# First attention of a vision tower: slot 0's exponential sums in halves, the last maxima behind them, and the value-weight scalings dealt out anew

## The reference, cut to what matters

```
q = einsum('bsc,oc->bso', x, Wq)      # 8 heads, 64 features each
k = einsum('bsc,oc->bos', x, Wk);  v = einsum('bsc,oc->bos', x, Wv)   # shared by the heads
scores = einsum('bhsd,bdt->bhst', q, k) / sqrt(8)
attn = softmax(scores, axis=-1)
ctx = einsum('bhst,btd->bhsd', attn, v)
out = einsum('bcp,oc->bop', ctx.transpose(0,2,1,3).reshape(b, H*KD, s), Wo)
```

## Time and profile before

| | |
|---|---|
| median of 3 runs | 71.36 us (71.33 to 71.44) |
| the profiled execution's own time | 71.47 us |
| its span, first to last instruction | 69.6 us |
| busy: TensorE / VectorE / ScalarE / GpSimd | 60.6 / 41.7 / 29.7 / 13.5 us |
| granted TensorE clock | 1.00 |
| scores of slot 0 to the end of `out0(3)` | 18.26 to 28.34 us |

### The profile page before, as it was taken

How to read it: one execution, slowest core, us unless ns; L and a number is a source line. 1 busy time by engine, 2 the same in 40 slices (tenths; PEclk the granted TensorE clock), 3 DMA queues, 4 the chain that set the end, 5 groups by cost and what they waited for, 6 DMA issues and landing times.

```text
span 69.6 us, 1990 instructions
## 1 busy us (share of the span) xinstructions
PE 60.6 (87%) x830; PEld 39.6 (57%) x839; DVE 41.7 (60%) x111; ACT 29.7 (43%) x69; POOL 13.5 (19%) x32
## 2 busy tenths in 40 slices
PE   3995896999999999999989995959999969989940
PEld 1330462787698578564448565548794318654910
DVE  2491039975699995535962546999563025756830
ACT  0240012431748852177764425259604283953030
POOL 6800039200000892058304000000000004000000
PEclk9999999999999999999999999999999999999999
DMA  0799999950000000000000000000000000000003
GB/s 0 182 381 370 392 225 243 235 175 0 0 9 0 0 0 9 0 0 5 0 0 0 0 9 5 0 9 0 0 9 0 0 0 0 0 0 0 0 0 75
DMA packets 2390, 4.07 MB, mean 58 GB/s; under 512 B 780, under 2 KB 1230, under 8 KB 2382
## 3 DMA queue, kind: packets, MB, share of 16 engines
q1 hardware_dynamic: 1568, 3.49, 17.4%
q10 hardware_dynamic: 781, 0.46, 2.2%
q0 software_dynamic: 32, 0.00, 0.0%
HBM read 3.82 MB, written 0.13 MB: 57 GB/s over the span
## 4 chain that ended last, share of the span: by engine, by line
PE 61%; DVE 12%; DMA 9%; ACT 7%; POOL 3%; issue 3%; DVEq 0%; ACTq 0%; POOLq 0%
DMA Xt<-in_x_dram 9%; PE psum L717 8%; PE psum L711 6%; DVE top L533 4%; ACT ge L457 3%; POOL WoS L300 3%; PE psum L727 3%; PE psum L928 3%; PE psum L974 3%; PE psum L819 3%; PE psum L770 3%; PE psum L1066 2%; PE psum L746 2%; DVE E L632 2%; DVE top L630 2%
## 5 line engine op out<-in xcount | busy, mean ns | idle before, releaser
L717 PE MATMUL psum<-warm 128*128 128x512 bf16 x44 | 14.5, 441 | 1.7 <-DVE warm L479 1.2
L717 PEld LDWEIGHTS psum<-warm 128*128 128x128 bf16 x53 | 5.2, 109 | 6.8 <-issue 3.6
L300 POOL TENSOR_TENSOR WoS<-pack_attn,top 128x256 f32<-128x256 f32 x5 | 3.1, 647 | 10.1 <-DVE top L540 10.1
L492 DVE TENSOR_TENSOR onehot<-idb,iota 128x2048 bf16<-128x2048 bf16 x4 | 4.8, 1241 | 0.0
L335 POOL TENSOR_TENSOR resT<-hT,xC 128x256 f32<-128x256 f32 x1 | 0.7, 724 | 20.0 <-DVE xC L661 20.0
L428 ACT ACTIVATE E<-E 128x512 f32<-128x512 f32 x4 | 2.5, 631 | 3.1 <-DVE E L632 3.1
L727 PE MATMUL psum<-Xt,pack_wp 128*64 128x256 f32 x16 | 2.2, 390 | 1.1 <-DMA Xt<-in_x_dram 1.1
L457 ACT ACTIVATE ge<-psum,pack_moe 128x512 f32<-128x512 f32 x4 | 2.5, 687 | 1.2 <-PE psum L1026 1.2
L711 PE MATMUL psum<-pack_ident,E 128*128 128x128 f32 x16 | 2.5, 276 | 0.7 <-DVE E L632 0.7
L630 DVE TENSOR_REDUCE top<-psum 128x8 f32<-128x512 f32 x4 | 2.7, 683 | 0.4 <-PE psum L943 0.4
L498 DVE TENSOR_TENSOR centre<-pack_ident,mean 128x128 f32<-128x128 f32 x1 | 0.3, 293 | 4.4 <-DMA pack_ident<-in_ident_dram 4.4
(11 more groups left out here) (206 smaller groups left out, 134.6 us busy)
## 6 DMA issues: line engine op xcount, KB each, us to landing
Xt<-in_x_dram SPq DMA_DIRECT2D x1, 1024.0 KB, 6.4
Xt<-in_x_dram SPq DMA_DIRECT2D x1, 512.0 KB, 7.4
pack_both<-in_both_dram SPq DMA_DIRECT2D x2, 240.2 KB, 8.8
pack_moe<-in_moe_dram SPq DMA_DIRECT2D x1, 450.0 KB, 9.8
pack_mid<-in_mid_dram SPq DMA_DIRECT2D x1, 327.5 KB, 9.7
pack_attn<-in_attn_dram SPq DMA_DIRECT2D x1, 288.0 KB, 8.0
pack_expert<-in_expert_dram SPq DMA_DIRECT2D x2, 130.0 KB, 9.4
pack_wp<-in_wp_dram ACTq DMA_DIRECT2D x1, 192.0 KB, 5.8
```

The source lines that it names most:

```text
L300: gp.tensor_tensor(WoS[:, s, 4 * u:4 * u + 4, :].rearrange("p (b n) d -> p b n d", b=2), bc(WoT[:, 2 * u:2 * u + 2, :], 1, 2), bc(top0[:, ...
L492: ve.tensor_tensor(onehot[:, 16 * k:16 * k + 16, :], bc(idb[:, k, :], 1, 16), iota16[:, :, :], ALU.is_equal).then_inc(s_hot, 1)
L717: mm(B[bank][:, :], lhsT=warm[:, 0:P], rhs=warm[:, :], start=True, stop=True)
```

## The change

Slot 0's eight exponentials signal after four and after eight. VectorE sums slot 0 in two halves of four heads, each with its own reciprocal, between the maxima of slot 2 and those of slot 3. So `softmax0_max(3)` stands behind both half sums. On TensorE `scores0(3)` moves behind `shift0(1)`. GpSimd scales slot 0's halves each after its own reciprocal, then both halves of slot 1, then slot 2 (first) and slot 3 (second). ScalarE scales slot 2 (second) rather than slot 1 (second), and does so after copying out slot 0's mix rather than before. VectorE keeps slot 3 (first) alone. Two of the three `keep_clock` products ahead of mix 0 go. The semaphore counts follow.

```diff
             def scaled_Wo(s, u, ready):
 
                 pool.wait_ge(s_rinv, ready)
...
-            scaled_Wo(0)
-            scaled_Wo(1)
-            scaled_Wo(2)
-            scaled_Wo(3)
+            scaled_Wo(0, 0, 1)
+            scaled_Wo(0, 1, 2)
+            scaled_Wo(1, 0, 3)
+            scaled_Wo(1, 1, 3)
+            scaled_Wo(2, 0, 4)
+            scaled_Wo(3, 1, 5)
...
-            for i in range(HEADS):
-                ins = sc.activation(E0[:, 0, i, :], B[i // 4][:, i % 4 * TOK:(i % 4 + 1) * TOK], ACT.Exp,
-                                    bias=shift[:, i:i + 1], scale=SC0)
-            ins.then_inc(s_exp0, 1)
+            for u in range(2):
+                for i in range(4 * u, 4 * u + 4):
+                    ins = sc.activation(E0[:, 0, i, :], B[i // 4][:, i % 4 * TOK:(i % 4 + 1) * TOK], ACT.Exp,
+                                        bias=shift[:, i:i + 1], scale=SC0)
+                ins.then_inc(s_exp0h, 1)
...
-            act.wait_ge(s_rinv, 2)
+            mixed(0)
+            act.wait_ge(s_rinv, 4)
             for i in range(4, HEADS):
-                ins = sc.activation(WoS[:, 1, i, :], WoT[:, 2 + i % 2, :], ACT.Copy, scale=top0[:, 2, 1, i:i + 1])
+                ins = sc.activation(WoS[:, 2, i, :], WoT[:, 2 + i % 2, :], ACT.Copy, scale=top0[:, 2, 2, i:i + 1])
             ins.then_inc(s_wosa, 1)
-            mixed(0)
...
             softmax0_max(2)
+            for u in range(2):
+                dve.wait_ge(s_exp0h, u + 1)
+                softmax0_sum(0, slice(4 * u, 4 * u + 4), u + 1)
             softmax0_max(3)
-            softmax0_sum(0)
             for s in range(1, SLOTS):
-                softmax0_sum(s)
-            for s, u in ((2, 1), (3, 0)):
-                dve.wait_ge(s_rinv, s + 1)
+                dve.wait_ge(s_exp0, s)
+                softmax0_sum(s, slice(0, HEADS), s + 2)
+            for s, u in ((3, 0),):
+                dve.wait_ge(s_rinv, 5)
...
             def mix0(s):
 
                 c, j = s // 2, s % 2
-                pe.wait_ge(s_exp0, s + 1)
-                pe.wait_ge(s_wos, s + 2)
-                if s == 1:
+                pe.wait_ge(s_wos, (2, 4, 5, 6)[s])
+                if s == 2:
                     pe.wait_ge(s_wosa, 1)
-                elif s >= 2:
-                    pe.wait_ge(s_wosd, s - 1)
+                elif s == 3:
+                    pe.wait_ge(s_wosd, 1)
...
             scores0(2)
+            shift0(1)
             scores0(3)
-            shift0(1)
             shift0(2)
             shift0(3)
+            pe.wait_ge(s_exp0h, 2)
+            keep_clock(0, 1)
+            mix0(0)
             pe.wait_ge(s_exp0, 1)
-            keep_clock(0, 3)
-            mix0(0)
-            pe.wait_ge(s_exp0, 2)
             keep_clock(2, 1)
             mix0(1)
             out0(0)
```

More of the change, by code:

```diff
@@ L210, in vit_tower @@
                                                sem("v0_ready"))
-        s_sc0, s_mx0, s_sub0, s_exp0 = sem("scores0_ps"), sem("max0_done"), sem("shifted0_ps"), sem("exp0_done")
+        s_sc0, s_mx0, s_sub0, s_exp0h, s_exp0 = (sem("scores0_ps"), sem("max0_done"), sem("shifted0_ps"), sem("exp0_half_done"),
+                                                  sem("exp0_done"))
         s_shift, s_wosa, s_gbar = sem("shift_ready"), sem("wos1_ready_act"), sem("gate_bar_ready")
@@ L294, in _, with scaled_Wo @@
                 pool.wait_ge(const_l1, 5 + u)
[L296 to L303, removed]
-            scaled_Wo(0)
-            scaled_Wo(1)
-            scaled_Wo(2)
-            scaled_Wo(3)
+            def scaled_Wo(s, u, ready):
+                pool.wait_ge(s_rinv, ready)
+                gp.tensor_tensor(WoS[:, s, 4 * u:4 * u + 4, :].rearrange("p (b n) d -> p b n d", b=2),
+                                 bc(WoT[:, 2 * u:2 * u + 2, :], 1, 2),
+                                 bc(top0[:, 2, s, 4 * u:4 * u + 4].rearrange("p (b n) -> p b n", b=2), 3, D),
+                                 ALU.mult).then_inc(s_wos, 1)
+            scaled_Wo(0, 0, 1)
[4 more added lines that the diff above has]
+            scaled_Wo(3, 1, 5)
             pool.wait_ge(in_expert, 32)
@@ L534, in softmax0_max, with softmax0_sum @@
                                  negate=True).then_inc(s_mx0, 1)
[L536 to L540, removed]
+            def softmax0_sum(s, heads, done):
+                ve.tensor_reduce(top0[:, 1, s, heads], E0[:, s, heads, :], X, ALU.add).then_inc(s_sum0, 1)
+                dve.wait_ge(s_sum0, done)
+                ve.reciprocal(top0[:, 2, s, heads], top0[:, 1, s, heads]).then_inc(s_rinv, 1)
             softmax0_max(0)
@@ L827, in out0 @@
                 pe.wait_ge(s_v0_ev, 1)
-                pe.wait_ge(s_exp0, 3)
+                pe.wait_ge(s_exp0, 2)
                 for b in range(2):
```

## The result

| | before | after |
|---|---|---|
| median | 71.40 us (71.33 to 71.47) | 72.14 us (71.96 to 72.28) |
| ratio after to before | | 1.0085 (1.0051 to 1.0119) |
| median and ratio, both kernels run again on another chip | 71.61 us | 72.03 us: 1.0064 (1.0041 to 1.0087) |
| span of the profiled execution | 69.6 us | 70.5 us |
| first product on image data | 7.26 | 7.64 |

What follows compares the result with a forecast made beforehand. Gapless TensorE work from mix 2 to the residual addition was taken to bound the kernel; mix 2, waiting for ScalarE's scalings, starts 0.33 late: 71.36 + 0.33 = 71.69, said as 71.7 us, range 71.25 to 71.95.

Steps and rivals of the forecast that it cites:

- Everything outside the stretch: Before the first maxima and from the residual addition on: nothing changes; the loss is simply added to a median of 71.36.
- The stretch: First attention, first maxima to residual addition: the addition moves from 28.46 to 28.79, 0.33 us later.
- the cost of coming back from scores 3 to shift 2: TensorE, return from 64x64 tiles to the full array: 0.10 for the mode change, then shift 2 takes 0.87.
- leaving out both drains: TensorE's two tile-mode changes around scores 3: without them the final sum would be about 0.1 smaller.
- Maxima 3 behind the half sums: VectorE: half sums of 0.42 each let maxima 3 start at 22.39; scores 3 allow the same time, taken as 22.40.
- GpSimd's head start isn't used: Before mix 0: GpSimd starts 0.97 us earlier, but TensorE arrives at 24.36 against 24.23 before.
- ScalarE ends the wait of mix 2: Mix 2: ScalarE's four scalings, behind its copy of mix 0, end at 26.31; mix 2 starts at 26.46, 0.33 late.
- At mix 1: GpSimd's two scalings of slot 1 end at 25.22; mix 1 starts at 25.37, while TensorE alone would allow 25.28.
- Rival (A): TensorE and VectorE: mode changes cost nothing and half sums don't hold the maxima; no slower, 71.43 us; chance 0.20.
- (B): Mix 1: GpSimd's two scalings of slot 1 decide at 0.78 each; mix 2 0.49 late, 71.85 us; chance 0.12.
- (C): Mix 0 and 1 use GpSimd's early start; mix 0 at 24.07, 0.16 earlier, 71.2 us; chance 0.13.
- (D): TensorE's clock drops to 1.2 GHz; the 4 us from mix 0 to out 3 take up to twice as long; chance 0.03.

Runs made afterwards that it cites:

- a_scores_first: Changed kernel with TensorE's order put back, scores 3 ahead of shift 1: ratio 1.0029 to the kernel before, first maxima to residual addition 9.63 us against 9.78.

## Why the prediction was right or wrong

The way was right, slower, and so was the chain of waits that led there. The time of 72.14 lies above the range, which ended at 71.95, and 0.45 above the forecast of 71.69. Two steps of the sum failed: the first makes up most of the error in the time, the second is the error in the stretch itself.

- *Everything outside the stretch*: the sum put it at nothing and set the loss on top of 71.36, the median of three runs within 0.11 us, with a measurement said to be good to 0.2%. The runs showed that this level isn't so steady. 27 runs of the same kernel on another chip lay between 71.36 and 72.23, with a median of 71.61, so 71.36 was at their lower end. The changed kernel had 72.03 there, again above the range. The difference between the two kernels in that comparison, 0.46, would have given 71.82. In the profiled executions of the first comparison, 0.38 of the 0.9 us are the image data landing later; for the other runs there is no profile, so what moved the medians stays open. This part is about 0.3 of the 0.45.
- *The stretch*: forecast +0.33, measured +0.43 twice. The step that failed is the cost of coming back from scores 3 to shift 2. The change of mode itself was 0.09 in (22.10 is 0.31 behind the last full product's 21.79) and close to the forecast out. But the first product after it holds the array for longer, as its 0.48 against 0.38 shows: shift 2 took 0.98 until shift 3's first product (22.72 to 23.70), not 0.87. The sum had 0.97 for shift 1, whose first product shows the same 0.48 in the earlier trace rows, and 0.87 for shift 2, though after the change it too is the first of its mode. That missing 0.1, with 0.04 of smaller differences, runs on: exponential 2 at 23.51 by the clock of before (forecast 23.37), mix 0 at 24.51 (24.36), mix 2 at 26.55 (26.46), the addition at 28.89 (28.79). ScalarE's copy followed mix 0 after 0.73, not 0.78, so 0.05 of the error was made up by luck. The Trainium skill's page "TensorEngine Tiling (Array Packing)", section Key Properties, says that a change of mode drains TensorE; the trace agrees, and here the drain with its slower first product was about 0.2 us per way back. The prediction's "about 0.1" for leaving out both drains doesn't follow from its own rows: without them shift 3 would have waited for maxima 3 until about 23.12 instead of 23.18, so its sum would have been 0.06 smaller.
- *Maxima 3 behind the half sums*: right, and scores 3 held them as well, as the forecast had it, in the end 0.1 longer. Half sums took 0.41 and 0.42 (0.42 forecast). The Trainium skill's page "VectorE: DVE Perf Modes", section on the TRN2 errata, gave an estimate of 0.33 by its row for an SBUF source, which the same section says comes out too low; the measured value agrees with that.
- *GpSimd's head start isn't used*: right, 1.0 us early, and 1.4 us of waiting for TensorE.
- *ScalarE ends the wait of mix 2*: right. The row says so, and taking two heads away gave back 0.23. What TensorE itself would have allowed was forecast at 0.21 earlier (26.25 against 26.46). At mix 1, where GpSimd was to come last by 0.09, TensorE's own list and GpSimd's scaling ended together: mix 1 stands 0.32 behind its `keep_clock` product, as mix 0 does with 0.31.
- *Rival (A)* fell with the mode changes of 0.09 and the half sums of 0.41, *(B)* because GpSimd's scalings of slot 1 ran at 0.57 and 0.61 each, *(C)* because TensorE reached mix 0 later than before, at 24.51 and not at 24.07, so that GpSimd's early scalings lay waiting, *(D)* because the stretch kept the full clock.

## What to carry to other kernels

A step that frees one engine early is worth nothing if the consumer's own list reaches the result later than before: read the list of the consumer first, then the time of the producer. Moving work ahead on an engine that feeds a chain (here half sums ahead of the last maxima) costs the whole chain behind it; the same half sums one place later were one of three parts of a version that gained 0.42 there. Which part gave how much wasn't measured. A forecast of an absolute time also needs the spread of the level that it starts from: about 0.3 of the 0.45 us of error came from there. And when a stage gets shorter and the time doesn't, look behind the stage for a new idle time marked issue before blaming the idea: here it took four instructions of padding to collect the gain.

## What the runs showed of the hardware

- VectorE had an idle time of 0.23 us, marked issue, at one place of its program: 0.52 from start to start instead of 0.20. Two instructions more ahead brought it there in the kernel before, four more took it off the path. The Trainium skill's page "Runtime: NRT & Kernel Launch", section Instruction fetch mechanics, says that an engine's instructions are refilled in blocks and that crossing a boundary is mostly hidden. The place agrees: a load of about 8 KB on queue 14 starts 0.67 us behind the instruction that follows the gap, in all three versions that have it, and moved with VectorE's program. That the engine stood still for a block that hadn't arrived isn't shown.
- After a change from 64x64 tiles to the full array the first product showed 0.48 us instead of 0.38, and the next one came 0.1 us later than in a steady stream. In `a_scores_first` the first product of shift 3 showed 0.48 after an idle time of 0.43 in the same mode, so it isn't the change of mode alone that brings this.
- The first product on image data lay between 7.09 and 7.64 us in nine profiles of kernels that are alike up to there.
